# A second wait ahead of GpSimd's gathers in a graph network's three gather passes

## The reference

```python
x = _layernorm(x + L0(x, edges))             # attention: segment softmax of 4 heads, weighted sum of h[src]
x = _layernorm(x + L1(x, edges, edge_attr))  # two convolutions: segment_max(x[src] @ W_msg + edge_attr @ W_edge, dst)
x = _layernorm(x + L2(x, edges))             # two layers with the mean of h[src] per destination
x = _layernorm(x + L3(x, edges))             # three layers with a degree-normed sum of h[src]
```

## Time and profile before

| | |
|---|---|
| median of 3 runs | 9821.23 us (9806.7 to 9841.38) |
| span of the profiled execution | 9705.1 us |
| busy: TensorE, VectorE, ScalarE, GpSimd | 4073.0, 5048.9, 2904.4, 4813.6 us |
| chain that ended last: VectorE, another core or unknown queue, TensorE, issue, GpSimd | 41%, 23%, 17%, 9%, 7% |
| TensorE's granted clock, mean of the span | 0.627 of full speed |

### The profile page before, as it was taken

How to read it: one execution, slowest core, us unless ns; L and a number is a source line. 1 busy time by engine, 2 the same in 40 slices (tenths; PEclk the granted TensorE clock), 3 DMA queues, 4 the chain that set the end, 5 groups by cost and what they waited for, 6 DMA issues and landing times.

```text
span 9705.1 us, 71574 instructions
## 1 busy us (share of the span) xinstructions
PE 4073.0 (42%) x19184; PEld 2488.5 (26%) x19184; DVE 5048.9 (52%) x10097; ACT 2904.4 (30%) x5669; POOL 4813.6 (50%) x5030
## 2 busy tenths in 40 slices
PE   1100000000444444344443344444444438999999
PEld 1000000000311111111112111111111118999999
DVE  4554444444456656565564565666565647522222
ACT  0222222222244444444442344444444420000000
POOL 6566667666166556555654665555555640000000
PEclk6555555555555555555555555555555559999999
DMA  4222222222133333333332333333333325567667
GB/s 124 70 82 77 75 74 80 74 77 73 28 104 109 103 99 111 96 103 99 103 103 70 101 107 97 103 105 101 103 101 100 106 73 202 212 235 262 226 236 251
DMA packets 642173, 1129.74 MB, mean 116 GB/s; under 512 B 164844, under 2 KB 422271, under 8 KB 641618
## 3 DMA queue, kind: packets, MB, share of 16 engines
q1 hardware_dynamic: 360112, 437.17, 14.5%
q0 software_dynamic: 159184, 251.10, 12.4%
q10 hardware_dynamic: 122578, 438.40, 11.4%
HBM read 713.46 MB, written 412.70 MB: 116 GB/s over the span
## 4 chain that ended last, share of the span: by engine, by line
DVE 41%; another core or an unknown queue 23%; PE 17%; issue 9%; POOL 7%; DMA 2%; ACT 1%; DVEq 0%; SPq 0%; POOLq 0%; ACTq 0%
DVE BUF L1537 9%; POOL CG L460 6%; PE psX L734 5%; PE psB L734 5%; PE psA L734 5%; DVE BUF L1532 4%; DVE XTQ L1563 4%; DVE STG L1563 4%; DVE BUF L1529 4%; DVE XTQ L1556 3%; DVE STG L1556 3%; DVE EX L1474 1%; PE psO L677 1%; DVE terms L1472 1%
## 5 line engine op out<-in xcount | busy, mean ns | idle before, releaser
L460 POOL DMA_INDIRECT CG<-table,BUF x4704 | 4484.3, 953 | 3031.4 <-DMA hist<-CG 1408.9
L1532 DVE TENSOR_SCALAR BUF<-iota,EG 128x392 bf16<-128x392 f16 x1568 | 528.9, 337 | 1880.0 <-remote 1617.1
L704 PE MATMUL psO<-WE,BUF 128*128 128x384 f32 x1568 | 1104.6, 858 | 313.2 <-DMA BUF<-in_edge_attr 197.3
L989 ACT ACTIVATE BUF<-iota,EG 128x128 bf16<-128x128 f16 x3136 | 958.1, 387 | 348.9 <-remote 139.4
L965 ACT COPY psX<-BUF 128x384 f32<-128x384 f32 x392 | 189.0, 482 | 2536.9 <-DVE XTQ L1563 1461.9
L777 PE MATMUL psA<-ident,F 128*100 128x128 f32 x1 | 0.5, 452 | 1893.9 <-DVEq L1439 1893.9
L486 POOL CAST CG<-EG x35 | 27.8, 794 | 1359.8 <-DVEq L1205 1359.8
L704 PEld LDWEIGHTS psO<-WE,BUF 128*128 128x128 f32 x1568 | 467.4, 320 | 736.2 <-issue 416.2
L713 PE MATMUL psB<-BUF 128*128 128x392 bf16 x523 | 240.7, 460 | 872.3 <-issue 616.6
L713 PE MATMUL psA<-BUF 128*128 128x392 bf16 x523 | 241.1, 461 | 851.5 <-issue 577.2
L713 PE MATMUL psX<-BUF 128*128 128x392 bf16 x522 | 241.0, 462 | 845.0 <-issue 592.4
(11 more groups left out here) (284 smaller groups left out, 7560.8 us busy)
## 6 DMA issues: line engine op xcount, KB each, us to landing
BUF<-counts SPq DMA_DIRECT2D x245, 784.0 KB
BUF<-counts ACTq DMA_DIRECT2D x245, 784.0 KB
counts<-BUF SPq DMA_DIRECT2D x1572, 98.0 KB
hist<-CG ACTq DMA_DIRECT2D x392, 384.0 KB
hist<-CG ACTq DMA_DIRECT2D x196, 416.0 KB
CG<-table,BUF POOLq DMA_INDIRECT x4704
BUF<-in_edge_attr SPq DMA_DIRECT2D x392, 128.0 KB
table<-TB SPq DMA_DIRECT2D x14, 336.0 KB
```

What stands on the lines that cost most here:

```text
L460: pool.indirect_dma_start(out=rows_in[:, u % RING, k, :], out_offset=None, in_=tab, in_offset=bass.IndirectOffsetOnAxis(ap=SRC[:, u * S + ...
L704: mm = pe.matmul(ETERM[:, s, a, 0:4 * DIM], EA[:, s, a, :], WE[:, m, :, :].rearrange("k c d -> k (c d)"), start=True, stop=True)
L989: far = nc.scalar.activation(FAR[:, j, a, :], iota16[:, 0:P], ACT.Square, bias=STEP[:, 2 + a, u * CS + j:u * CS + j + 1], scale=-1.0)
L1532: ts(RHS[:, j, 1, :], iota16[:, :], STEP[:, 1, n:n + 1], None, ALU.is_equal).then_inc(onehot_ready, 1)
```

## The change

Ahead of the gathers of slot u, for u of 2 and more, GpSimd waits for `scanned` at q * 196 + u - 1, which is the end of the scan of slot u-2 of the same pass. The wait for the ring's place stays. All else is the same.

```diff
             for u in range(2 if q == 0 else 0, SLOTS):
                 r, lap = u % RING, q * LAPS + u // RING
+                if u >= 2:
+                    pool.wait_ge(scanned, q * SLOTS + u - 1)
                 if u >= RING:
                     pool.wait_ge(hist_stored[r], 16 * lap)
                 gather_slot(u, tab, rows_in)
```

## The result

The changed kernel takes 10,666.9 us (median of 4 runs, 10,660.8 to 10,672.3), the kernel before 9814.0 us (4 runs, 9806.7 to 9841.4): ratio 1.087, 95% interval 1.084 to 1.090, or 853 us more. The forecast was 10,370 us in a range of 9,800 to 10,920. Its main case had a range of its own, 10,100 to 10,650, and the result lies 17 us above that.

What follows compares the result with a forecast made beforehand. No engine was full: GpSimd's gathers set a limit of 10.0 us a slot, with waits for late signals above it. Pass 0 +1075 and passes 1 and 2 -527 gave +548 on 9821: 10,370 us, range 9,800 to 10,920.

Steps and rivals of the forecast that it cites:

- main case: Whole kernel: pass 0 loses 1075 us, passes 1 and 2 gain 527 us; 10,370 us, chance 0.58.
- VectorE's path: Pass 0, from L1465 to the end of scan u: 5.45 us of each 16.8 us slot.
- The early slots: Pass 0, slots with 24 us waits at L1328 in table work: +20 us taken, bounds 0 and +60.
- late signals: Semaphore releases coming long after the raising instruction ended; 24 us waits at L1328 vanish if they were such.
- late phase: Stretch of late signals, some 20 us into a gather burst until 3 us after GpSimd idles; none expected in pass 0.
- the walk through one cycle: Passes 1 and 2: late phase catches slot s+4, four slots in 46.5 us, 11.6 us a slot, -527 us.
- rival A': Passes 1 and 2: late phase catches slot s+3, three slots in 45 us, +800, 11,700 us; chance 0.06.
- rival A: Passes 1 and 2: no gain, 12.9 us a slot as now, 10,896 us; chance 0.20.
- B: Passes 1 and 2: no late phase at GpSimd's pace, 10.0 to 10.2 us a slot, 9724 us; chance 0.13.
- Theory F: Late signals come from fast 8 us slots of VectorE, ScalarE and TensorE beside gathers; B's claim, chance 0.13.
- C: Whole kernel: the new wait is already met and changes nothing, 9821 us; chance 0.03.
- The port lock: VectorE two-port modes and GpSimd exclude each other; waits end within one 0.94 us gather, so L1532's 14.26 us isn't this.

Runs made afterwards that it cites:

- the larger memset: GpSimd memset of 128x256 behind each gather, on the kernel before without the new wait: 9043.3 us against 8141.8, in a set without late signals.
- the memsets: GpSimd memset of 128x64 behind each gather, on the kernel before without the new wait: ratio 0.947 with late signals, 1.020 without.

## Why the prediction was right, and where it was off

**Pass 0** was forecast at 16.8 us a slot and +1075 us, and measured at 16.94 us and +1081. The mechanism is the one that was forecast; that the total comes within 6 us is in part luck. Its terms: eight gathers 8.73 (measured 8.74), landing 2.55 (2.52), VectorE's path 5.45 (5.38), the new wait 0.05 (0.28). The wait had no row in the trace of before, and its true size is next to the upper bound taken from the step between two gathers, 0.3 us, not next to the value that I chose. The error of 0.23 x 195 = 45 us was partly made up by the shorter path (14 us), the landing (6 us) and the last interval, which has no gathers ahead of it and took 4.5 us (12 us).

The early slots had been given +20 us for the 24 us waits at L1328. These waits vanished, as late signals, yet the first 40 intervals together are 17 us longer than the later ones, so the term was right in size and wrong in cause. Some 14 of the 17 us are in the gathers themselves: those beside VectorE's table work take 1.3 to 2.5 us instead of 0.94. One of them, with VectorE's two instructions beside it:

```profile
381.87 1.07 DVE L1298 TENSOR_SCALAR BUF<-EG 128x1792 int32<-128x1792 int32 x1
382.98 1.09 DVE L1299 CAST CG<-BUF 128x1792 bf16<-128x1792 int32 x1
...
382.23 1.96 POOL L460 DMA_INDIRECT CG<-table,BUF  x1 [7.31 <-DVE STG L1496]
```

Also right: bursts of eight with 7 us of rest bring no late phase, in three profiles of pass 0 under the new wait. Two of them count, since their other passes had late signals; the third had none anywhere.

**Passes 1 and 2** were forecast at 11.6 us a slot, -527 us, and gave 12.6, -128 between the two profiles of the record and -277 in those of the later set (2602 + 2615 against 2466 + 2475). The step that failed is the walk through one cycle. The scans come 8.0, 15.8, 32.2 and 51.0 us after the cycle's start; the walk had 8, 15, 25 and 46.5. The late phase catches the steps of slot s+3 as well as s+4: the wait of 4.05 us ends at 4516.45, 22 us after the burst's start, and there the steps of s+3 were still to be done. The prediction named this as rival A' ("its steps end only 1 us before 20 us"), but priced it at 45 us for three slots; both slots were caught in turn, each for a part, and the cost lies between. In the walk GpSimd then gathered 32 in one run and fell idle at 40 us; in the trace the late scan s+3 held it for 2.13 us after 24 gathers, and it fell idle at 42. The 12.6 us a slot are nearer to rival A's 12.9 than to the forecast's 11.6. The direction was right, and the run with the wait in passes 1 and 2 alone shows it by itself, -212 us.

**The rivals.** A (no gain there) is excluded by that run's interval, 0.977 to 0.983. B (no late phase in passes 1 and 2 under the new wait) is excluded where there are late signals, since they came all the same. Theory F isn't tested by these passes, for in the cycle above two scans at 8 us still stand ahead of the late waits. Pass 0 of the kernel before speaks against it: four scans 9.7 to 10.3 us apart, paced by the gathers, end from 1475.32 to 1505.42, and the next one waited 2.34 us for a late signal. Faster ones at 5.3 and 8.1 us stand further back, so F is made unlikely and not excluded. C, no change at all, is excluded by the result.

**The sum against the clock.** I added the change to the median, as if the 116 us between the median and the profiled span were a constant share outside it. They aren't. For the profiled execution of the changed kernel the time is 10,660.8 us with a span of 10,658.9, 1.9 us outside. The kernel before scatters between executions, 9778 to 9893 us for its copy, and the profiled one, about 9707 us by the same 1.9 us, was shorter than all of these; what made it so was not looked into. Counted from its own time, the forecast of the span was 9705 + 548 = 10,253 against 10,659, off by 406 us: 399 from passes 1 and 2, 6 from pass 0. Against the median, 10,667 instead of 10,370, the error is 297 us; the other 109 are hidden by the short execution.

**The port lock** of the Trainium skill (SBUF — State Buffer, "Who interferes with whom"), under which a wait ends with the other engine's instruction: no run here shows it as the cause of the long waits. In the sets without late signals the same one-hot rows run beside an unbroken run of gathers, and passes 1 and 2 hold GpSimd's pace of 10.0 us, so whatever the lock costs is hidden there; with late signals the wait of 14.26 us in the earlier trace rows spans 11 whole gathers. The slow gathers beside table work in early pass 0 are of the size of such a wait: the one shown ends 0.1 us behind L1299. No run here changes that work, so the lock as their cause isn't shown.

**What stays open.** The mechanism of the late signals, and why they are there in three sets of runs (9814, 9850 and 9829 us for the kernel before) and absent in two (8139 and 8142 us), where nothing of the kernel differs. Dense gathers alone don't bring them, for in the sets without them GpSimd issues 1568 gathers in one run at the same 1.25 us. The chip's number was 9 in one set with them, 5 in one without, and 1 in two sets, one with them and one without; whether two chips bear that number isn't known to me, so chip and time aren't told apart. The wait for slot u-3 met no late signals and is unknown with them; so is the larger memset. No version tried beats the kernel before everywhere: the wait in passes 1 and 2 alone comes nearest, 2.0% faster with late signals and the same to 0.1% without, and the memsets are 5.3% faster with them and 2.0% slower without.

## What to carry to other kernels

Before limiting how far a producer runs ahead, lay its start and the consumer's end on one line in program order: where the consumer takes the next slot's data first (pass 0: logits of u+1 ahead of scan u), a limit of two slots is a limit of one, and the two engines take turns; where it takes them last (passes 1 and 2), the same limit costs nothing. The time of a slot is then the sum of both engines' parts (here 16.9 us), and the loss is this sum less the pace that the longer part alone would give (10.0 us); the sum could be read to 1% from two slots of the timeline. Set a kernel's time beside the pace of its slowest engine (here 10.0 us a slot, from a row): a gap of 30% filled by waits for signals whose senders had long ended belonged here to the conditions of a run, and a comparison holds for the set of runs in which it was made.

## What the runs showed of the hardware

- The same program took 8139 us in one set of runs (the copy with the wait in passes 1 and 2 alone as well) and 9850 us in another, with nearly the same busy times: VectorE was busy 5156 us in the profile of 8141.9 us that is shown above, GpSimd 4822, against 5048.9 and 4813.6 in the span of 9705.1 us. The difference is waits for semaphores whose senders ended earlier, as in the first profile: up to 15.6 us at the one-hot line, 1 to 3 us between VectorE's own instructions.
- Such late signals were seen only under long runs of gathers, 1.25 us apart without the memsets and a little more with them. In pass 0 with bursts of eight gathers and 7.3 us of rest there is none, in two profiles whose other passes have them. A rest of 4 us doesn't end them: in pass 0 of the kernel before, bursts of eight with 4.0 to 4.3 us of rest stand in the slots of 14.00 us.
- In pass 0 of the kernel before, 42 of the 195 intervals from scan to scan are 14.00 us to 0.01 us, mostly two to five in a row (in a later profile 45, to 0.08 us).
- From the end of a VectorE scan to the start of the waiting gather on GpSimd it is 0.28 us.
- A gather took 0.94 us on GpSimd, and up to 2.5 us beside VectorE's table work in pass 0 (1.96 us beside a 128x1792 copy of 1.09 us that changes int32 to bf16).
